# Queries, keys and values in DRAM: one layout for queries and keys, values without ones, and ScalarE interleaving the values in the attention stage

## What is computed

```python
xn = _layernorm(x)
# attention: 16 heads of 16 columns, window 128
q, k, v = xn @ Wq.T + bq, xn @ Wk.T + bk, xn @ Wv.T + bv
scores = where(mask, einsum('bqhd,bkhd->bhqk', q, k) * SCALE, -10000.0)
attn = softmax(scores) + 1e-9
ctx = einsum('bhqk,bkhd->bqhd', attn, v)
# experts: the best 2 of 8 by xn @ gate_w.T + beta, plus a shared expert
x = x + ctx @ Wo.T + bo + experts(xn) + shared(xn)
```

## Time and profile before

| | before |
|---|---|
| median of 3 runs | 2066.87 us (2055.52 to 2069.42) |
| profiled execution | 2073.88 us, span on the core 2071.9 us |
| PE, DVE, ACT, POOL busy | 83%, 54%, 44%, 39% of the span |
| queue of SyncE (q1) | 202368 packets, 261.44 MB, 46.3% of 16 DMA engines |

### The profile page before, as it was taken

How to read it: one execution, slowest core, us unless ns; L and a number is a source line. 1 busy time by engine, 2 the same in 40 slices (tenths; PEclk the granted TensorE clock), 3 DMA queues, 4 the chain that set the end, 5 groups by cost and what they waited for, 6 DMA issues and landing times.

```text
span 2071.9 us, 38865 instructions
## 1 busy us (share of the span) xinstructions
PE 1728.1 (83%) x11609; PEld 1421.9 (69%) x11610; DVE 1129.1 (54%) x3465; ACT 905.9 (44%) x1737; POOL 808.9 (39%) x757
## 2 busy tenths in 40 slices
PE   6936545550999999999999988889899999899987
PEld 6925535540888888888888865666666666666666
DVE  6653232331666666666666665565565655555552
ACT  2312111111555554545455435555555655555553
POOL 0024332340000000000000026788788888888886
PEclk9998777775999999999999968899888998998998
DMA  8447766765444444444444447666677767777752
GB/s 281 141 146 220 226 208 203 221 212 191 148 147 147 145 149 151 152 152 152 152 152 152 129 102 146 145 161 154 146 157 153 166 158 160 152 160 154 155 125 75
DMA packets 254491, 333.80 MB, mean 161 GB/s; under 512 B 26992, under 2 KB 172656, under 8 KB 252400
## 3 DMA queue, kind: packets, MB, share of 16 engines
q1 hardware_dynamic: 202368, 261.44, 46.3%
q0 software_dynamic: 12288, 33.57, 6.5%
q10 hardware_dynamic: 39792, 38.28, 5.5%
HBM read 210.52 MB, written 112.72 MB: 156 GB/s over the span
## 4 chain that ended last, share of the span: by engine, by line
PE 54%; SPq 14%; issue 12%; DMA 10%; POOL 4%; ACT 3%; DVE 2%; another core or an unknown queue 0%; ACTq 0%; POOLq 0%; DVEq 0%
PE psum L148 31%; PE psum L783 11%; SPq L576 7%; DMA plain_arena<-xn_d 4%; DMA split_arena<-k_d 4%; PE psum L1227 4%; PE psum L1267 2%; PE psum L1250 2%; SPq L811 2%; PE psum L854 2%; SPq L813 2%; ACT plain_arena L1369 1%; POOL split_arena L1169 1%; POOL plain_arena L1152 1%; DMA plain_arena<-y_d,b_ix 1%
## 5 line engine op out<-in xcount | busy, mean ns | idle before, releaser
L148 PE MATMUL psum<-split_arena 128*128 128x512 f32 (+1 forms) x4560 | 996.0, 374 | 20.4 <-POOL split_arena L1169 10.8
L148 PEld LDWEIGHTS psum<-split_arena 128*128 128x128 f32 x4560 | 787.4, 201 | 159.3 <-POOL split_arena L1169 17.0
L1462 DVE CUSTOM_DVE_ANT_0 plain_arena<-psum,mask 128x256 f32<-128x256 f32 (+1 forms) x1024 | 340.2, 386 | 306.0 <-PE psum L1227 276.8
L1369 ACT ACTIVATE plain_arena<-psum 128x512 f32<-128x512 f32 (+1 forms) x512 | 250.8, 543 | 322.4 <-PE psum L1250 282.9
L1212 POOL MEMSET plain_arena<- 128x256 f32 x1 | 0.3, 312 | 699.0 <-ACTq L137 699.0
L783 PE MATMUL psum<-split_arena 128*128 128x256 f32 x1872 | 233.8, 285 | 0.0
L1227 PE MATMUL psum<-split_arena 48*128 48x256 f32 (+1 forms) x1024 | 169.8, 356 | 70.1 <-DMA split_arena<-k_d 44.9
L783 PEld LDWEIGHTS psum<-split_arena 128*128 128x128 f32 x1872 | 226.9, 192 | 0.1
L1227 PEld LDWEIGHTS psum<-split_arena 48*128 48x128 f32 x1024 | 106.1, 205 | 149.3 <-issue 71.8
L613 POOL DMA_INDIRECT sorted_d<-plain_arena,q_idx x128 | 124.2, 970 | 206.1 <-DVE q_idx L700 170.4
L900 ACT ACTIVATE plain_arena<-psum 128x512 f32<-128x512 f32 x156 | 93.3, 598 | 219.3 <-PE psum L148 219.1
(11 more groups left out here) (132 smaller groups left out, 1946.7 us busy)
## 6 DMA issues: line engine op xcount, KB each, us to landing
plain_arena<-in_gate_w SPq DMA_DIRECT2D x39, 512.0 KB, 5.1
plain_arena<-in_up_w SPq DMA_DIRECT2D x39, 512.0 KB, 6.2
plain_arena<-in_down_w SPq DMA_DIRECT2D x39, 512.0 KB, 7.0
plain_arena<-sorted_d SPq DMA_DIRECT2D x39, 512.0 KB, 3.9
y_d<-plain_arena ACTq DMA_DIRECT2D x39, 512.0 KB, 3.6
plain_arena<-in_x SPq DMA_DIRECT2D x32, 512.0 KB, 3.9
plain_arena<-xn_d SPq DMA_DIRECT2D x32, 512.0 KB
q_d<-split_arena SPq DMA_DIRECT2D x64, 256.0 KB
```

The lines of the kernel that those rows point to most:

```text
L148: last = pe.matmul(out, lhs_t(p), rhs(q), start=(begins and c == 0 and k == 0), stop=(ends and c == len(chunks) - 1 and k == 2), skip_grou ...
L1369: act.activation(b_pt[:, g % 2, 2 * p + par, 4 * half:4 * half + n, :].rearrange("p k s -> p (k s)"), psum[:, 2 + par, 0:n * P], ACT.Exp, ...
L1462: last = dve.tensor_tensor_reduce(b_junk[:, 2 * par + i % 2, 0:cols], psum[:, par, at:at + cols], mask[:, 2 * P - cols:2 * P], -1.0, 3e38, ...
```

## The change

`q_d` and `k_d` become one layout (channel, part, row), where keys have their low part first. A batch is stored in four transfers of 512 KB that begin with 128 partitions, instead of eight of 256 KB. `load_qk` reads the same bytes in as many transfers, with rows of the same 2 KB; the 32 partitions that hold both parts now alternate between parts, in q as in k. `v_d` holds values only, 512 KB for a batch instead of 1 MB. In the attention stage they go to a new tile `b_vd`, in rows of 256 bytes, and ScalarE copies them at lag 12 into the even numbers of `b_v` (128 x 256, four times a turn); TensorE's `values` waits for that copy (`b_vc`) instead of the load. GpSimd sets the ones in `b_v` once, at the start of the attention stage, and TensorE and VectorE wait for all three of its memsets there (`b_zeroed`); before, TensorE did not wait for memsets and VectorE for one. The memset of `q_v` and the waits for it go.

```diff
-    q_d = nc.dram_tensor("q_d", (B, H, 2, DH, S), F32).ap()
-    k_d = nc.dram_tensor("k_d", (B, H, 2, DH, S), F32).ap()
-    v_d = nc.dram_tensor("v_d", (B, P, T, 2 * D), F32).ap()
+    q_d = nc.dram_tensor("q_d", (B, D, 2, S), F32).ap()
+    k_d = nc.dram_tensor("k_d", (B, D, 2, S), F32).ap()
+    v_d = nc.dram_tensor("v_d", (B, P, T, D), F32).ap()
...
-                        for m in range(KD):
-                            sp.dma_start(dram[ds(b, 1), m * 2 * HG:(m + 1) * 2 * HG, part, :, :].rearrange(
-                                "o h d s -> (o h) d s"), q_qk[:, u, k, part, m, :].bitcast(F32)).then_inc(q_st[u], 16)
+                        sp.dma_start(dram[ds(b, 1), :, part if k == 0 else 1 - part, :].rearrange(
+                            "o (m p) s -> p (o m) s", p=P), q_qk[:, u, k, part, :, :].bitcast(F32)).then_inc(q_st[u], 16)
...
-            pool.memset(q_v[:, :, :, :, :, 1].rearrange("p u a h d -> p (u a h d)"), 1.0).then_inc(q_one, 1)
...
-                    dve.tensor_tensor(q_v[:, u, 2 * h:2 * h + 2, :, :, 0],
-                                      psum[:, 6 + h, :].rearrange("p (a h d) -> p a h d", a=2, h=H),
-                                      bv_sb[:, :].rearrange("p (h d) -> p h d", h=H).unsqueeze(1).to_broadcast(
-                                          [P, 2, H, DH]), ALU.add).then_inc(q_vb, 1)
+                    dve.tensor_tensor(q_v[:, u, 2 * h:2 * h + 2, :], psum[:, 6 + h, :].rearrange("p (a d) -> p a d", a=2),
+                                      bv_sb[:, :].unsqueeze(1).to_broadcast([P, 2, D]), ALU.add).then_inc(q_vb, 1)
...
-                for dram, tile, once, both in ((q_d, b_q, 0, 16), (k_d, b_k, 32, 0)):
-                    heads = dram[ds(b, 1), g * HG:(g + 1) * HG, :, :, :].rearrange(
-                        "o (p q) w d s -> q (o w d) p s", q=2)[par]
-                    sp.dma_start(tile[at + once:at + once + 16, g, :, :].bitcast(F32), heads[0:DH]
-                                 ).then_inc(b_ldqk[g], 16)
-                    sp.dma_start(tile[at + both:at + both + 32, g, :, :].bitcast(F32), heads
+                for k, (dram, tile) in enumerate(((q_d, b_q), (k_d, b_k))):
+                    rows = dram[ds(b, 1), g * 64:(g + 1) * 64, :, :].rearrange(
+                        "o (p q d) w s -> q (o d) w p s", q=2, d=DH)[par]
+                    sp.dma_start(tile[at:at + 16, g, :, :].bitcast(F32), rows[:, k, :, :]).then_inc(b_ldqk[g], 16)
+                    sp.dma_start(tile[at + 16:at + 48, g, :, :].bitcast(F32), rows.rearrange("d w p s -> (d w) p s")
...
-                hold_after(sp, b_pv, 4 * b + g - 1)
-                sp.dma_start(b_v[:, s, :, :], v_d[ds(b, 1), :, :, g * P:(g + 1) * P].rearrange(
+                hold_after(sp, b_vc, 4 * b + g - 1)
+                sp.dma_start(b_vd[:, s, :, :], v_d[ds(b, 1), :, :, g * 64:(g + 1) * 64].rearrange(
...
+            pool.memset(b_v[:, :, :, :, 1].rearrange("p s a c -> p (s a c)"), 1.0).then_inc(b_zeroed, 1)
...
-                pe.wait_ge(b_ldv[s], 16 * (2 * b + g // 2) + 16)
+                pe.wait_ge(b_vc, 4 * b + g + 1)
...
+            pe.wait_ge(b_zeroed, 3)
...
+            def interleave_values(b, g):
+                s = g % 2
+                act.wait_ge(b_ldv[s], 16 * (2 * b + g // 2) + 16)
+                after(act, b_pv, 4 * b + g - 1)
+                act.copy(b_v[:, s, :, :, 0].rearrange("p a c -> p (a c)"), b_vd[:, s, :, :].rearrange("p a c -> p (a c)")
+                         ).then_inc(b_vc, 1)
...
-            dve.wait_ge(b_zeroed, 1)
+            dve.wait_ge(b_zeroed, 3)
```

More of the change, by code:

```diff
@@ L1421, in turn @@
                         exponentials(b, r)
+                    b, g = due_group(t, h, 12)
+                    if b is not None:
+                        interleave_values(b, g)
                     b, g = due_group(t, h, LAG_U)
```

25 lines of the change are left out of this document (12 added, 13 removed).

## The result

| | before | after |
|---|---|---|
| median of the runs of one comparison | 2062.47 us (2055.52 to 2069.42, 4 runs) | 1936.93 us (1935.94 to 1939.10, 4 runs) |
| ratio | | 0.9393, 95% interval 0.9354 to 0.9431 |
| profiled execution's span | 2071.9 us | 1936.0 us |
| step of the projection stage (batch 1 to 15) | 22.1 us | 15.1 us |
| projection stage ends (first load of the experts) | 501.9 us | 383.6 us |

The kernel is 6.1% faster, 125.5 us by the medians. The two spans differ by 135.9 us, since the profiled execution of before took 2073.9 us, longer than each of the four in the table. Those 135.9 us are 118.3 of the projection stage and 18.5 of the attention stage, less 0.9 of the experts.

A forecast was written before the change was run, and what follows sets the result against it. Stores of q and k on half the DMA engines were taken to bound the projection stage. Stage -118, its end -11, copy +3, value loads -2, memsets +1.6 make -126 us, from 2066.9 to 1941 us; range 1900 to 1988.

The forecast's parts named there:

- The cause, 8 of 16 engines: Projection stage: old q and k stores use 8 of 16 DMA engines, new ones 16; 6.9 us a batch instead of 13.8.
- The rate of 16 engines: Projection stage: q and k stores run at twice the rate, 288 to 322 GB/s; scatters taken at 310.
- TensorE 10.5 us and GpSimd 10.2 us are floors, both below 13.7: Projection stage: both engines' own steps are shorter than the transfers' 13.7 us, so the transfers still set the step.
- above 15: Sign of being wrong: a projection-stage step above 15 us or below 12 us; 13 to 14 expected.
- The tail: Projection stage's end, last batch's stores to the experts' first load: 29.5 us shrinks by about 11 us.
- The copy: Attention stage: ScalarE's 64 copies of values go into its waits; costs 3 us, bounds nothing and 33.
- The memsets: Start of attention stage: TensorE now waits for three memsets, costing about 1.6 us.
- The halved loads of values: Attention stage: smaller value loads let the q and k loads behind them go sooner; gains 2 us, between 0 and 10.
- The engines catch up sooner: Rival, 15%: stores run better than twice as fast, TensorE or GpSimd set a step of 10.5 to 12 us; about 1905.
- One engine stays behind: Rival, 17%: something fixed per batch on one DMA engine limits stores to 230 GB/s; step 16 us, about 1977.
- The stores do not spread: Rival, 5%: only the smaller value stores gain, 1.3 us a projection step; 2051 us.
- the fear that DRAM takes alternating rows badly: Rival, 4%: q and k stores to alternating 2 KB rows fall to 110 GB/s; step 25.9 us, 2120 us.

The follow-up runs named there:

- the pause: Full change, with GpSimd pausing after the fourth of a batch's eight scatters until VectorE has added the bias to the first half of its values: 1916.68 us, ratio 0.9313.
- mean of 12 against mean of two: Attention stage: 12 executions with the change of the values (11 kernels), mean 853 us, against before and q and k alone, 866 and 861 us.
- the padded kernel: Full change, but an unused row pair after each head's 16 in DRAM makes the stores eight of 8 x 16 x 512 again: 2029.37 us, ratio 0.9850.
- the values alone: Kernel before with only the values without ones and ScalarE's copy; queries and keys keep the old layout and eight stores: 2034.68 us, ratio 0.9893.

## Why the prediction was right, and where it was not

**What bounds the kernel: right.** The stores of q and k set the projection stage. The kernel with their layout alone has its whole gain.

**The cause, 8 of 16 engines: right, and shown.** With the order of rows and the number of issues held, 8 at the front gives a share of 0.50 and a step of 19.9 us, 128 at the front a step of 15.1. More than nine packets of these stores were under way at once in 0.6% of their time there and in 79% here. The rule of the Trainium skill (DMA: Bandwidth & Descriptors, "Why a DMA increments its semaphore by 16 and not by 1") that the slowest dimension of both sides decides how many engines carry a transfer held in both kernels.

**The rate of 16 engines: too low.** I doubled 144 to 161 GB/s to 288 to 322 and took 310 for the scatters. Measured are 357 to 364 in stretches of after and 373 over twelve steps without scatters. The transfers of a step need 11.2 us at that rate, and 11.9 by the share of 0.79 in after, where my sum has 13.7.

**"TensorE 10.5 us and GpSimd 10.2 us are floors, both below 13.7": this step failed.** It took the engines as running side by side, so that the step would be the longest of the three. They are links of one circle: GpSimd's burst waits for VectorE's indices, which stand behind VectorE's work on values, which waits for signals of TensorE, and these come late as long as GpSimd scatters. The circle is 9.9 + 4.8 us in the step shown, and 15.1 in the mean. The two errors, 1.8 to 2.5 us too much for the transfers and 4.6 us too little for the engines' 10.5, partly cancel: 13.7 predicted, 15.1 measured. That is just outside the 12.5 to 14.9 that I named, and by my own mark ("above 15") this part was wrong, if only by the execution that was profiled: the same kernel again had 14.9. The trace of before had the signs in its first batches, where nine signals up to 184 us were late, by up to 6.1 us; two of them lie in the very step from 150.09 to 160.57 us that I took as TensorE's own. The circle's links are read from the trace; of the edits to it only the pause shows in the times, and taking the indices out of it does not.

**The tail: too small.** I took 11 us for the time between the last batch's stores and the next stage. It went from 29.5 us to 9.8, so 19.7. SyncE no longer stands in its own queue there: the stores of q and k are issued in 3.1 us. Together the stage gave 14 x 7.0 + 19.7 = 118 us, where I had 129.

**The copy: 3 us, measured nothing.** It takes 0.43 us (I said 0.4), and the copy made twice costs nothing that can be measured.

**The memsets: 1.6 us, measured 1.8.**

**The halved loads of values: under-sized.** I said 2 us, bounds 0 and 10. The stage became some 10 us shorter (mean of 12 against mean of two), and TensorE's wait for k 13 us in the mean, at the end of my bounds. The nearest landing, 4.9 us, fell to 4.3, and 0.6 us in each of 19 places is 11 us. My bound was worked out rightly, but I took a value near its lower end for want of a reason. I also named 866 us within 10 as the sign for this stage, which the 847 us of the profiled execution and the mean of 853 miss. The Trainium skill's figure (DMA: Bandwidth & Descriptors, "Specifications") of 512 bytes for full line rate showed as a small loss only: a packet of 256 bytes took 20 ns where one of 512 took 35, so 0.57 of its time and not all of it, as I had feared. The landing of k behind the loads of values did not get longer, and TensorE's wait for k fell in all 12 traces.

**The rivals.** "The engines catch up sooner" had the rate of the stores right, but GpSimd and TensorE did not give 10.5 to 12. "One engine stays behind" had the step nearly right (16 us), by a mechanism that is not there: the share is 1.02 to 1.03 in the stretches of stores. "The stores do not spread" describes the padded kernel: 2029 us, where I had 2051. Of the fear that DRAM takes alternating rows badly no kernel shows anything: the padded kernel has that order and is no slower than the values alone.

So it is luck that the median (1941 forecast, 1937 measured) came out closer than its parts: the projection stage gave 11 us less than I said, the attention stage 13 (mean of the 12 against that of the two without the new values) to 21 us (the profiled executions) more.

## What to carry to other kernels

Look at the first number of a transfer's shape on the DRAM side and at the DMA share of a stretch in which it alone runs: here a queue that was held back at a share of one half was a layout to change, not a bandwidth that was used up. When a bound is taken away, don't take the largest of the remaining engines' own times as the next one; follow who waits for whom round one step, since a chain of short waits through three engines can be longer than any of them. And where a burst on one engine delays the others' signals, a pause in it can be worth more than it costs.

## What was not expected of the hardware

While GpSimd issued indirect DMAs one after another, 38 of 76 signals of TensorE reached their semaphore over 0.6 us late, the latest 7.9 us, and mostly several at once, from 1.4 us after the burst's end. Without the scatters all 96 came within 0.02 us, at a higher DMA share (1.04). What in a scatter holds the signals up, its descriptors, its writes or something else on their way, was not tried and stays open. In before, where the stores kept 8 engines busy, the same bursts held up one of 28 signals once the stores set the step (from 190 us on). So here it took the scatters and DMA engines that were all busy beside them; that is a comparison of a few kernels, and no proof.

An issue on SyncE whose transfer finds room takes 0.37 us in the median, and 2.0 us where the queue is held back. The time of an issue is thus itself a sign of how far behind the transfers are.
